# A transformer block on one core: q written to scratch in the row order of k, three writes instead of six, the head in another order, the second query read on another queue

## What is computed

```python
x = L0_attn_x                                   # (4, 1024, 128) float32
mod = (_silu(L0_c) @ L0_wmod).reshape(4, 6, 1, -1)
sa, ca, ga, sb, cb, gb = ...                    # six vectors of 128 for each batch
h = _layernorm(x) * (1 + ca) + sa
# attention: 16 heads of 8 columns, over a reshape, not a transpose
qkv = (h @ Wqkv.T + bqkv).reshape(B, 16, S, 24)
q, k, v = jnp.split(qkv, 3, axis=-1)
attn = softmax(einsum('bhsd,bhtd->bhst', q, k) / sqrt(8))
vals = einsum('bhst,bhtd->bhsd', attn, v).reshape(B, S, 128)
x = x + ga * (vals @ Wo.T + bo)
h = _layernorm(x) * (1 + cb) + sb
# 8 experts, the two best of each token weighted, with the router's probability as bias
x = x + gb * ffn(h, router_w, expert_weights)
```

## Time and profile before

| | us |
|---|---|
| median of 3 runs (lowest, highest) | 556.71 (555.5, 557.04) |
| the profiled execution | 557.98 |
| its span, first to last instruction | 556.1 |
| TensorE busy | 519.1 (93%) |
| ScalarE busy | 494.8 (89%) |
| VectorE busy | 362.8 (65%) |
| GpSimd busy | 219.2 (39%) |

### The profile page before, as it was taken

How to read it: one execution, slowest core, us unless ns; L and a number is a source line. 1 busy time by engine, 2 the same in 40 slices (tenths; PEclk the granted TensorE clock), 3 DMA queues, 4 the chain that set the end, 5 groups by cost and what they waited for, 6 DMA issues and landing times. The chain is left out here.

```text
span 556.1 us, 14357 instructions
## 1 busy us (share of the span) xinstructions
PE 519.1 (93%) x4064; PEld 215.3 (39%) x4064; DVE 362.8 (65%) x1271; ACT 494.8 (89%) x571; POOL 219.2 (39%) x429
## 2 busy tenths in 40 slices
PE   7488889999999999999999999999999999999983
PEld 6233333334343434343433333343434343433352
DVE  4435457677867666677767667677676666664466
ACT  1279989999999999999999999999999999998962
POOL 1223233344443334444443343444433344443335
PEclk9999999999999999999999999999999999999997
DMA  4573333333333333333333333333333332333010
GB/s 100 128 199 90 89 96 78 77 97 88 89 90 89 96 98 84 76 78 93 88 90 90 98 93 83 72 88 91 88 89 95 98 86 65 91 96 84 17 32 14
DMA packets 85497, 48.44 MB, mean 87 GB/s; under 512 B 61508, under 2 KB 76240, under 8 KB 85456
## 3 DMA queue, kind: packets, MB, share of 16 engines
q1 hardware_dynamic: 70162, 43.07, 30.0%
q10 hardware_dynamic: 15294, 4.82, 3.8%
HBM read 32.91 MB, written 14.94 MB: 86 GB/s over the span
## 5 line engine op out<-in xcount | busy, mean ns | idle before, releaser
L547 ACT ACTIVATE probs<-ps_scores 128x1024 f32<-128x1024 f32 x512 | 485.8, 1028 | 42.9 <-DMA q_scr<-qk_parts 19.6
L735 PE MATMUL ps_attn<-probs,values 128*32 128x512 f32 x2048 | 248.1, 599 | 0.4 <-issue 0.4
L717 PE MATMUL ps_scores<-query_stack,key_stack 32*128 32x512 f32 x1024 | 130.7, 500 | 17.5 <-ACT probs L547 11.4
L717 PEld LDWEIGHTS ps_scores<-query_stack,key_stack 32*128 32x128 f32 x1024 | 49.4, 183 | 167.9 <-ACT probs L547 164.1
L422 POOL TENSOR_SCALAR var_eps<-moments 128x1 f32<-128x1 f32 x64 | 12.3, 192 | 222.7 <-DVE moments L1078 149.5
L735 PEld LDWEIGHTS ps_attn<-probs,values 128*32 128x32 f32 x2048 | 54.0, 109 | 110.5 <-issue 110.3
L765 PE MATMUL ps_side<-experts_gated,h2T 128*128 (+1 forms) x228 | 74.7, 409 | 0.0
L1067 DVE RECIPROCAL sums_inv<-sums 128x128 f32<-128x128 f32 x32 | 30.5, 952 | 32.5 <-DMA attnT<-a_scr 32.5
L1074 DVE TENSOR_TENSOR x<-ps_side,x_gated 128x128 f32<-128x128 f32 x31 | 9.0, 292 | 60.8 <-PE ps_side L765 57.2
L1150 DVE TENSOR_TENSOR weighted<-ps_side,coef 128x256 f32<-128x256 f32 x114 | 46.5, 408 | 2.4 <-PE ps_side L765 2.4
L471 POOL TENSOR_TENSOR mix<-weighted 128x512 f32<-128x512 f32 x31 | 39.7, 1280 | 0.0
(11 more groups left out here) (129 smaller groups left out, 498.9 us busy)
## 6 DMA issues: line engine op xcount, KB each, us to landing
key_stack<-k_scr SPq DMA_DIRECT2D x128, 128.0 KB, 2.7
query_stack<-q_scr SPq DMA_DIRECT2D x121, 64.0 KB, 2.2
q_scr<-qk_parts SPq DMA_DIRECT2D x188, 32.0 KB, 2.0
k_scr<-qk_parts SPq DMA_DIRECT2D x64, 64.0 KB, 1.7
a_scr<-attn ACTq DMA_DIRECT2D x126, 18.0 KB
sums<-a_scr SPq DMA_DIRECT2D x32, 64.0 KB, 2.1
attnT<-a_scr SPq DMA_DIRECT2D x32, 64.0 KB, 2.2
out_dram<-out_all ACTq DMA_DIRECT2D x29, 64.0 KB, 1.8
```

The costliest lines, as they stand in the source:

```text
L547: nc.scalar.activation(probs[:, k % RING, g, :], ps_scores[:, slot(k, g), :], ACT.Exp, scale=SCALE)\
L717: mm = nc.tensor.matmul(out_, key_stack[p0:p0 + 32, parity, 2 * k:2 * k + 2, :].rearrange("p j r -> p (j r)"), query_stack[p0:p0 + 32, par ...
L735: mm = nc.tensor.matmul(ps_attn[q:q + 32, :], values[:, parity, g, k, :], probs[:, k % RING, g, h * HALF:(h + 1) * HALF], start=(k == 0), ...
```

## The change

q gets the row order of k (`(d j)`: column by column, the 16 tokens inside). The weights `wqkT` are copied out of PSUM with one instruction rather than two, the bias of q is loaded with one DMA like that of k, the matrix that sums over a head (`head_sum`) is one, not two, and `write_q` is three DMAs of 128 partitions; the bytes written are the same. `read_q` reads the same bytes with other strides. In the head, the value projection of tile 1 goes to another PSUM bank (`ps_scores`), so that the bias add no longer waits for it; GpSimd's squares of tile 1 wait for `qk_parts_done`; VectorE does hT of tile 2 before the statistics of tile 3 and `setup_columns`; the transpose of tile 3, the norms of tile 2, their maximum and hT of tile 3 move into the first tile; 14 products of `keep_warm` are added in six places; and the read of tile 2's query stacks moves from ScalarE's first tile to SP's prologue, ahead of the rest of x.

```diff
     k_scr = nc.dram_tensor("k_scr", [G, 2, P, R], F32, kind="Internal").ap()
-    q_scr = nc.dram_tensor("q_scr", [2, G, 3, P // 2, R], F32, kind="Internal").ap()
+    q_scr = nc.dram_tensor("q_scr", [G, 3, hd, 2, JH, R], F32, kind="Internal").ap()
     a_scr = nc.dram_tensor("a_scr", [J, hd + 1, G, R], F32, kind="Internal").ap()
...
         qk_parts = sb("qk_parts", [P, 2, 2, P], F32R)
-        head_rows = sb("head_rows", [P, 2, J])
-        head_sum = sb("head_sum", [P, 2, J], F32R)
+        head_rows = sb("head_rows", [P, J])
+        head_sum = sb("head_sum", [P, J], F32R)
         squares = sb("squares", [P, 2, P], F32R)
...
-        def write_q(eng, n1, copies=range(6)):
+        def write_q(eng, n1, copies=range(3)):
...
             reached(eng, q_loaded, loaded_before)
-            for h in range(2):
-                rows = qk_parts[h * R:(h + 1) * R, 0].bitcast(F32).rearrange("p a (g r) -> p a g r", g=G)
-                for place, a in enumerate((0, 1, 0)):
-                    if 3 * h + place not in copies:
-                        continue
-                    eng.dma_start(q_scr[h, :, place].rearrange("g p r -> p g r"), rows[:, a]).then_inc(q_written, 16)
+            rows = qk_parts[:, 0].bitcast(F32).rearrange("p a (g r) -> p a g r", g=G)
+            for copy, a in enumerate((0, 1, 0)):
+                if copy in copies:
+                    eng.dma_start(q_scr[:, copy].rearrange("g d h i r -> (d h i) g r"), rows[:, a]).then_inc(q_written, 16)
...
         def read_q(eng, n1, parity, stacks=range(4)):
-            q_count, scores_before = times(eng, n1, 96), times(eng, plus(eng, n1, -2), 1)
+            q_count, scores_before = times(eng, n1, 48), times(eng, plus(eng, n1, -2), 1)
             reached(eng, scores_ready[KT - 1][G - 1], scores_before)
...
                     p0 = 64 * g + 32 * h
-                    parts = q_scr[h, g].rearrange("s (d i) r -> (s d) (i r)", d=hd)
-                    rows = bass.AP(tensor=parts.tensor, offset=parts.offset, ap=[[HALF, 2 * hd], [hd * HALF, 2], [1, HALF]])
+                    parts = q_scr[g, :, :, h].rearrange("s d i r -> (s d) (i r)")
+                    rows = bass.AP(tensor=parts.tensor, offset=parts.offset, ap=[[2 * HALF, 2 * hd], [2 * hd * HALF, 2], [1, HALF]])
                     eng.dma_start(query_stack[p0:p0 + 32, parity].bitcast(F32).rearrange("p i r -> p (i r)"), rows).then_inc(q_loaded, 16)
...
             sp.dma_start(wqkv_in[:], Wqkv.rearrange("(k p) i -> p k i", p=P)).then_inc(w_loaded, 16)
-            bias_parts = bqkv.rearrange("(h i c d o) -> c h d i o", h=2, c=3, d=hd, o=1)
-            for h in range(2):
-                sp.dma_start(bqk_cols[h * R:(h + 1) * R, 0:1], bias_parts[0, h], allow_slow_non_contiguous=True).then_inc(bias_cols_loaded, 16)
-            sp.dma_start(bqk_cols[:, 1:2], bqkv.rearrange("(j c d o) -> c d j o", c=3, d=hd, o=1)[1],
-                         allow_slow_non_contiguous=True).then_inc(bias_cols_loaded, 16)
+            bias_parts = bqkv.rearrange("(j c d o) -> c d j o", c=3, d=hd, o=1)
+            for which in range(2):
+                sp.dma_start(bqk_cols[:, which:which + 1], bias_parts[which], allow_slow_non_contiguous=True).then_inc(bias_cols_loaded, 16)
             sp.dma_start(bqkv_rows[:], bqkv.partition_broadcast(P)).then_inc(bqkv_loaded, 16)
...
             def prologue():
                 write_k(1)
-                write_q(sp, 1, (4, 5))
+                write_q(sp, 1, (2,))
                 read_k(1, 0)
...
                 read_k(2, 1)
+                read_q(sp, 2, 1)
...
             rstd(1, moments1, var_eps1, rstd1, "moments1_done", "var1_done", "rstd1_done")
+            reached(pool, ev["qk_parts_done"], 1)
             squares_of_tile(1)
...
                         router(plus(act, t, -2))
-                    if k == 3 and before == 0:
-                        read_q(act, 2, 1)
                 if before == 4:
...
-            write_q(act, 1, (0, 1, 2, 3))
+            write_q(act, 1, (0, 1))
             read_q(act, 1, 0, (0, 1, 2))
...
                 nc.tensor.transpose(ps_attn[:, 0:B], c_in[:], ident[0:B, 0:B]).then_inc(setup_pe, 1)
-                keep_warm(2)
+                keep_warm(3)
                 pe.wait_ge(w_loaded, 16)
...
-            def a_project_v(u1, ring, col):
+            def a_project_v(ps, u1, ring):
...
                     for odd in range(2):
-                        mm = nc.tensor.matmul(ps_side[odd * R:(odd + 1) * R, col + n * R:col + (n + 1) * R],
+                        mm = nc.tensor.matmul(ps[odd * R:(odd + 1) * R, n * R:(n + 1) * R],
                                               hT[:, ring, n * R:(n + 1) * R], wvT[:, odd].rearrange("p k d -> p (k d)"),
...
                 for n in range(2):
-                    mm = nc.tensor.matmul(ps[:, n * J:(n + 1) * J], squares[:, n, :], head_sum[:, n, :], start=True, stop=True)
+                    mm = nc.tensor.matmul(ps[:, n * J:(n + 1) * J], squares[:, n, :], head_sum[:], start=True, stop=True)
                 mm.then_inc(ev["norms_done"], 1)
...
                 if before >= 2 and after >= 1:
-                    a_project_v(at[2], 1 - parity, P)
+                    a_project_v(ps_side[:, P:2 * P], at[2], 1 - parity)
                 if past < 4 <= before:
...
                 if before < 2:
-                    a_project_v(at[2], 1 - parity, 2 * P)
+                    a_project_v(ps_side[:, 2 * P:3 * P], at[2], 1 - parity)
                 if past < 3 <= before:
...
                     scores(at[0], at[1], parity, 0, False)
+                if before == 0:
+                    reached(pe, ev["qkT_done"], 2)
+                    a_transpose(3)
+                    a_norms(ps_side[:, P + NE:P + NE + 2 * J], 2)
                 for k in range(0, KT, 2):
...
             a_transpose(1)
+            keep_warm(2)
             pe.wait_ge(setup_dve, SETUP_WQKV)
             a_project_qk(1, 0)
-            a_project_v(1, 0, 2 * P)
+            a_project_v(ps_scores[:, 2, HALF:HALF + P], 1, 0)
             setup_columns()
+            keep_warm(2)
             reached(pe, ev["qkT_done"], 1)
...
             a_norms(ps_scores[:, 1, 0:2 * J], 1)
+            keep_warm(1)
             a_normT(ps_scores[:, 1, HALF:HALF + P], 1)
+            keep_warm(4)
             a_transpose(2)
             a_project_qk(2, 1)
-            reached(pe, ev["qkT_done"], 2)
-            a_transpose(3)
-            a_norms(ps_side[:, P + NE:P + NE + 2 * J], 2)
+            keep_warm(4)
             tiles(pe, tile)
...
             def a_qk_parts(n, n1):
...
-                k_count, q_count = times(dve, n, 32), times(dve, n, 96)
+                k_count, q_count = times(dve, n, 32), times(dve, n, 48)
                 reached(dve, ev["qkT_done"], n1)
...
-            def a_values(u1, ring, col):
+            def a_values(ps, u1, ring):
                 reached(dve, ev["v_ps_done"], u1)
                 v.scalar_tensor_tensor(out=values[:, ring, :, :, 0:hd],
-                                       in0=ps_side[:, col:col + P].rearrange("p (g k d) -> p g k d", g=G, d=hd),
+                                       in0=ps.rearrange("p (g k d) -> p g k d", g=G, d=hd),
                                        scalar=VALUE_SCALE, in1=spread(bv[:], 1, G), op0=ALU.mult, op1=ALU.add)\
...
                     exact_maxima(t, at[1], parity)
+                if before == 0:
+                    a_norm_max(ps_side[:, P + NE:P + NE + 2 * J], 2)
+                    a_hT(2, 3, 0)
                 written0(at, before, after, past)
...
                 if before >= 2 and after >= 1:
-                    a_values(at[2], 1 - parity, P)
+                    a_values(ps_side[:, P:2 * P], at[2], 1 - parity)
                 if past < 3 <= before:
...
                 if before < 2:
-                    a_values(at[2], 1 - parity, 2 * P)
+                    a_values(ps_side[:, 2 * P:3 * P], at[2], 1 - parity)
                 if past < 3 <= before:
...
             def prologue():
...
                 a_hT(0, 1, 0)
-                dve.wait_ge(bias_cols_loaded, 16 * 3)
-                reached(dve, ev["v_ps_done"], 1)
+                dve.wait_ge(bias_cols_loaded, 16 * 2)
                 a_qk(1)
...
                 value_bias()
-                a_values(1, 0, 2 * P)
+                a_values(ps_scores[:, 2, HALF:HALF + P], 1, 0)
                 head_sums()
...
                 a_bounded(ps_scores[0:1, 1, HALF:HALF + P], 1, 0)
+                a_hT(1, 2, 1)
                 a_moments(2, 3)
                 setup_columns()
-                a_hT(1, 2, 1)
                 a_qk(2)
...
                 a_xhat(2, 3)
-                a_norm_max(ps_side[:, P + NE:P + NE + 2 * J], 2)
-                a_hT(2, 3, 0)
...
             def head_sums():
                 dve.wait_ge(ident_ready, 1)
-                v.tensor_reduce(head_rows[:, 0].rearrange("p (h i) -> p h i", h=2),
```

(9 more changed lines are left out.)

## The result

The changed kernel takes **552.87 us** (median of 6 runs, 552.51 to 553.11) against 557.22 us for the kernel before in the same comparison (6 runs, 555.5 to 557.5). The ratio is 0.9925, with an interval from 0.9909 to 0.9941. The profiled execution took 553.11 us with a span of 551.3; before it was 557.98 and 556.1. The forecast of 551.1 lay 1.8 too low, its range holds the result, and rival (a), at 553.3, lies nearest.

The account below looks back on a forecast made before the run. ScalarE's 512 exponentials (485.8 of 556.1 us) were taken to bound the kernel. The 17th exponential at 36.7 instead of 42.80 gains 6.1, less 0.5 for x: net 5.6, median 551.1 us, range 549.3 to 552.6.

Parts of the forecast that it names:

- rival (a): In the head TensorE's clock stays low: 17th exponential at 39.3, gain 3.4 us, median 553.3; chance 0.27.
- Step 1: In the head, earlier bias add and shorter subtraction: q and k parts of tile 1 ready about 10.6, not 11.45.
- Step 2: Scratch trip of tile 1: ScalarE's query reads at 13.6 to 14.7, SP's at about 15.6, in by 18 to 18.6.
- Step 3: TensorE's work before the first scores: they begin at 19.7 to 20.7, taken as 20.2, against 23.01.
- the cover of flag and branch: Ahead of the first scores, fillers can hide the flag's load and branch; 1.0 to 1.1 us if uncovered.
- Step 4: In the first tile, work moved between scores 0 and 1 makes a new wait, costing 0.7 us (0.5 to 1.0).
- Step 5: In the first tile, taking four query reads off ScalarE shrinks the 2.48 us gap before the ninth exponential, saving 1.7.
- The loop: From the 17th exponential to the end of the span, the same 513.3 us; a move over 1 means wrong.
- The rest of x: Load for the second tile, issued at 28 to 28.5, landing about 40; gives back 0.5 us (0 to 1.0).

Follow-up runs that it names:

- e7: Changed kernel with step 1 undone: value projection back in the shared PSUM bank, GpSimd's squares not held behind the parts; 553.51 us.
- e3: Kernel before with only q's new row order, three writes, one weight copy, one bias load and one head sum; 555.62 us.
- e4: Changed kernel with transpose of tile 3, norms of tile 2, their maximum and hT of tile 3 back ahead of the first tile; 552.61 us.
- e2: Changed kernel with the four query reads of tile 2 back on ScalarE's queue behind the eighth exponential; 552.21 us.
- e5: Kernel before, unedited, profiled a second time; 557.23 us, one execution.
- e6: Changed kernel, unedited, profiled a second time; 555.13 us, one execution.
- e8: Changed kernel with seven more filler products where TensorE stood idle, in the head and first tile; 553.32 us.
- e9: e8 with the rest of x loaded by two DMAs, one tile first and then the other 27; 553.09 us.
- e11: Changed kernel with the edits of e8, e9 and e10 together; 553.17 us.
- e12: e11 with x loaded as four tiles ahead of the first tile, then eight behind SP's reads in each of the first three; 561.69 us.
- e10: Changed kernel with the load of the experts' weights moved behind the query writes of tile 2; 553.95 us.

## Why the prediction was right

The range held, and the direction; the sum under it didn't hold in all its terms.

**Step 1 was right.** Bias add at 9.48 (9.4 forecast), subtraction 0.43 (0.3 to 0.5), parts at 10.70 (10.6). The subtraction took 0.72 with the squares beside it (before, and again in e7), so it did stand still for GpSimd. The Trainium skill ("SBUF — State Buffer", "SBUF: two separate sides") has it so for a VectorE instruction with two SBUF inputs, and the traces agree, 0.72 against 0.43.

**Step 2 was right but for its end.** A q write costs 0.49, the cheap end of my bounds and the row I had called nearest; ScalarE's reads began at 13.64 (13.6). SP's read went at 15.92 (15.6), but it landed at 19.0, not by 18 to 18.6: the landing of 3.1 was longer than the 2.8 of before.

**Step 3 gave 20.68 where I took 20.2**, and 20.68 is the end that I had called slow. The mis-sized term was the cover of flag and branch: I took it as mostly hidden, and at 1.0 to 1.1 if not. I let fillers hide it because products hide it in the loop; but in the head the wait for the read stands in front of the flag's load, so nothing behind it can be hidden: 1.6 us from landing to scores, ten times over. Right was that the order of TensorE and VectorE ceased to bind: of the 2.3 us by which the first exponential moved, e3 has 0.1 and e4 1.66.

**Step 4 was right**: 0.51 where I took 0.7 (0.5 to 1.0). Not foreseen was that it may take back all that the move saves (e4).

**Step 5 failed as a cause.** I booked 1.7 us for taking four reads off ScalarE. e2 puts them back and loses nothing; the 2.48 us had in them slow issues (2.29 for two, 1.19 elsewhere, and in e5 the same gap was 1.61) that were gone in e3 with the three saved writes on SP, and behind it TensorE was late anyway. The waits of 0.80 and 1.60 that I had tied to the clock stayed, since the clock stayed low.

**Rival (a) is what happened.** Its scores at 20.7 (20.68), first exponential at 21.5 (21.51), seventh waiting 0.8 (0.80). Its 17th at 39.3 became 39.97, mostly because the weighing at the low level cost 1.60 and not 0.8: a gain of 2.83 instead of 3.4. (By its own terms, 21.5 + 17.7 = 39.2, that rival's gain was 3.6 and its time 553.1; the sum had slipped by 0.2.) The chance of 0.27 looks too small. The forecast leaned on fillers with gaps between them. Of the six traces with just these 14 fillers, four have the first scores at 0.80 and two at 0.51, and in none did the upper level hold until the gates.

**The loop was wrong by 2 in the first trace.** I had said that it would take the same 513.3 us from the 17th exponential on; it took 551.3 - 39.97 = 511.3, and that was my own mark for being wrong. The difference is the single stalls (2.79 against 0.85 us), whose places move with the program and whose sizes change from run to run. In the second traces it took 555.4 - 42.17 = 513.2 (e5) and 553.3 - 39.67 = 513.6 (e6), so there the loop was as forecast. Rival (a)'s own mechanism, with 2.8 instead of 3.4, would have given 553.9 (556.71 - 2.83), which lies in the range too. That fewer stalls brought the median down to 552.87 fits the traces, but most of the runs have no trace, and it isn't shown for them; about 1.5 of the 4.35 us between the two medians stays argued. That the total came as near to (a)'s 553.3 as it did is partly luck: the head gave less than (a) had, and something that neither it nor the forecast had booked gave the rest.

**The rest of x** cost nothing in the changed kernel: issued at 29.88 (28 to 28.5 forecast), it landed at 39.0, and VectorE came at 40.30 behind TensorE. Had the forecast come true, it would have: in e8 the head was 2.8 faster, and all of it was waited for again in the second tile, where I had booked 0.5 with 1.0 at most. So 551.1 looks out of reach for this kernel even with the clock up.

## What to carry to other kernels

When a wait stands ahead of a load of a flag and a branch, their cost (here 1.6 us) is added to whatever is waited for, and work put in front of the wait hides nothing of it; look at which semaphore that instruction waits for last, not at how busy the engine is before it. Before booking the whole of a gap to the instructions in it, look at what would have been late without them: the gap of 2.48 us (1.61 in the second trace) was worth nothing on one side (e2) and 0.8 to 1.7 on another (e3). And before speeding up a head, list the loads that are hidden only because the head is slow; here 2.8 us were lost again while one load of 28 tiles of x was landing, partly by a wait for its data and partly by a stall of an engine that didn't need the data at all. And count a stall of TensorE twice: where its clock fell behind one, the next weighing took 2.96 to 3.47 us instead of 1.92 (e6, e8, e9).

## What the hardware showed that I had not expected

**A large load beside a branch.** While 27 or 28 tiles of x were landing (9.2 to 10.7 us), TensorE stood 2.0 to 2.6 us in issue at one branch of the second tile (e8 to e11), though its semaphores were there in e9 and e11. From the row transpose ahead of that branch to the scores behind it these four took 2.31 to 2.91 us. The ten others took 1.17 to 1.30, of which 0.84 to 0.97 is the wait for the buffer, and in all ten nothing of x was landing: it had landed before (at 39.0 in the changed kernel, whose transpose came at 39.86), and in e12 one piece had landed and the next wasn't issued yet. So the stall proper is 1.0 to 1.7 us. In e11 from 35 to 39 us the queue that carries instructions moved two packets (packets, MB, share of 16 engines):

```profile
q8 instruction: 2, 0.03, 4.2%
```

What is waited for may be the program itself, behind the packets of x. The traces don't show it: no row says what a packet of that queue was for, none moved within the gap of e11 (35.8 to 38.2) or of e9 (37.4 to 39.7), and e12 moved one from 36.6 on, ahead of the same branch, without a stall. Nor does it help with the single stalls of about 1 us in the unrolled tiles: most are within 2 us of such a packet, but this queue moved 15 of them from 20 to 120 us in the changed kernel, so that something is always near.

**The clock in the head is not decided by the program alone.** The same 14 fillers left the first scores at 0.80 us (changed, e6, e2, e7) or lifted them to 0.51 (e4, e10); with seven more, four of them inside the first tile, all of e8, e9, e11 and e12 had 0.50 or 0.51, and three of them kept the upper level through the gates and the first weighing, which none with the 14 alone did. The plainest case is one kernel against itself: the changed kernel had the upper level at about 8 us in e6, lost it before 10 and regained it at about 30, and in its first trace had it for the first time at about 31.4. The Trainium skill, "TensorE: Matmul & The Clock Gate", section "What's actually happening", says that the point of the rise varies by half a microsecond to either side from run to run of one kernel. The traces agree that it varies, but by far more: beside that case, 15.7 us in e4 for the same fillers, and over 1 us between two traces of the kernel before. And the printed clock is not to be trusted in the head. The table of stretches gives these two (us from the start, length, busy time and instructions of PE, PEld, DVE, ACT and POOL, granted clock, DMA share, GB/s), first of the changed kernel, then of e6:

```profile
20.00:24.00 4.00, 2.63 (x12) 1.51 (x12) 1.19 (x7) 1.98 (x3) 0.00 (x0) 1.00 0.38 85
```

```profile
20.00:24.00 4.00, 2.53 (x12) 1.51 (x12) 0.99 (x5) 1.94 (x2) 0.00 (x0) 0.50 0.37 81
```

In both the scores take 0.80 us. Only the second prints the lower level.
